# Two qkv blocks of the next image between the last turns of an image, and an own reciprocal root

## What is computed

```python
def _gn(v, G=32, eps=1e-5):
    g = v.reshape(B_, G, C_ // G, H_, W_)
    m = jnp.mean(g, axis=(2, 3, 4), keepdims=True)
    s = jnp.var(g, axis=(2, 3, 4), keepdims=True)
    return ((g - m) / jnp.sqrt(s + eps)).reshape(v.shape)

proj = xw @ W_qkv + b_qkv                   # q, k, v of every pixel
logit = jnp.einsum('npc,nqc->npq', q_win * SCALE, k_win)   # window means
topk_logit, r_idx = jax.lax.top_k(logit, TOPK)             # 4 windows of 49
attn = jax.nn.softmax(jnp.einsum('bmqc,bmkc->bmqk', q_h * SCALE, k_sel), axis=-1)
o = jnp.einsum('bmqk,bmkc->bmqc', attn, v_sel)
out = (o + lepe) @ W_o + b_o                # lepe: 3x3 depthwise conv of v
x = x + out
```

## Time and profile before

| | us |
|---|---|
| median of 3 runs | 3751.95 |
| lowest, highest | 3751.21, 3754.92 |
| the profiled execution's own time | 3752.41 |
| its span in the profile | 3750.6 |
| first layer, to about | 1650 |
| PE, DVE, ACT, POOL busy | 3507.4, 2372.2, 2143.5, 1659.6 |

### The profile page before, as it was taken

One profiled execution on the slowest core, in us unless ns is written; L12 is line 12 of the kernel. 1 busy time (PEld: TensorE's weight loads), 2 busy tenths in 40 slices (PEclk: granted clock), 3 DMA queues, 4 the chain that ended last, 5 costly groups with the idle time before them and its releaser, 6 DMA issues. The chain is left out here.

```text
span 3750.6 us, 107535 instructions
## 1 busy us (share of the span) xinstructions
PE 3507.4 (94%) x31974; PEld 2975.0 (79%) x31974; DVE 2372.2 (63%) x6267; ACT 2143.5 (57%) x5921; POOL 1659.6 (44%) x2575
## 2 busy tenths in 40 slices
PE   6989898989899999969999999999999969979999
PEld 4656565656566565669999999999999969979998
DVE  5868787777778786843333333333333359988898
ACT  5979797888888797944443333333333324345554
POOL 2736364645556464710003333333334436646665
PEclk8999999999999999989999999999999979989999
DMA  6232332323141423211110000000001200000000
GB/s 219 69 99 74 92 82 89 85 64 105 59 113 48 120 56 115 59 67 50 50 46 0 0 0 0 0 0 0 0 12 62 62 21 1 1 25 24 35 35 35
DMA packets 202870, 194.34 MB, mean 52 GB/s; under 512 B 35744, under 2 KB 191136, under 8 KB 199456
## 3 DMA queue, kind: packets, MB, share of 16 engines
q1 hardware_dynamic: 171168, 177.15, 15.2%
q10 hardware_dynamic: 31360, 12.87, 1.3%
HBM read 123.30 MB, written 66.58 MB: 51 GB/s over the span
## 5 line engine op out<-in xcount | busy, mean ns | idle before, releaser
L196 PE MATMUL bank<-h,w_hh 128*128 128x128 f32 x8032 | 933.8, 275 | 0.0
L196 PEld LDWEIGHTS bank<-h,w_hh 128*128 128x128 f32 x8032 | 917.0, 192 | 0.0
L241 ACT ACTIVATE h<-bank,bg 128x128 f32<-128x128 f32 x1008 | 370.1, 367 | 818.7 <-PE bank L196 818.6
L1582 ACT ACTIVATE Pr<-bank,nmx 128x256 f32<-128x256 f32 x1568 | 722.6, 477 | 110.4 <-DVE nmx L1700 96.7
L1521 POOL TENSOR_TENSOR Pr<-Pr,rden 128x768 f32<-128x768 f32 x392 | 574.7, 1466 | 389.4 <-DVE rden L1767 389.4
L1700 DVE TENSOR_REDUCE nmx<-bank 128x1 f32<-128x256 f32 x1568 | 556.2, 416 | 207.5 <-PE bank L1868 204.8
L287 DVE SCALAR_TENSOR_TENSOR inp<-bank,b_in,tz 128x256 f32<-128x256 f32 x196 | 85.8, 479 | 696.4 <-ACT tz L224 696.4
L1513 POOL COPY kg<-kT 128x64 f32 x1568 | 315.0, 244 | 341.3 <-DMA row<-ix 187.0
L1879 PE MATMUL bank<-ident,Pr 128*128 128x128 f32 x3136 | 449.8, 284 | 16.5 <-DVE Pr L1756 9.6
L1591 ACT ACTIVATE PT<-bank 128x512 f32<-128x512 f32 x784 | 427.2, 604 | 36.4 <-PE bank L1879 33.8
L1879 PEld LDWEIGHTS bank<-ident,Pr 128*128 128x128 f32 x3136 | 338.6, 142 | 116.0 <-issue 74.4
(11 more groups left out here) (265 smaller groups left out, 6497.9 us busy)
## 6 DMA issues: line engine op xcount, KB each, us to landing
v_rows<-v_padded SPq DMA_DIRECT2D x168, 232.0 KB, 3.3
vg<-v_windows SPq DMA_DIRECT2D x1176, 32.0 KB, 2.0
first_gates<-gate_sums SPq DMA_DIRECT2D x28, 512.0 KB, 2.6
gate_sums<-first_gates SPq DMA_DIRECT2D x28, 512.0 KB, 3.6
v_padded<-vpad SPq DMA_DIRECT2D x56, 232.0 KB, 2.1
X<-in_x SPq DMA_DIRECT2D x8, 1568.0 KB, 15.2
vg<-v_windows ACTq DMA_DIRECT2D x392, 32.0 KB, 2.7
x_backup<-X SPq DMA_DIRECT2D x8, 1568.0 KB, 6.0
```

Source lines behind the costliest of these rows:

```text
L196: ins = pe.matmul(bank[m][:, tt * COLS:(tt + 1) * COLS], w_hh[:, k, m * 128:(m + 1) * 128], prev[:, k, :], start=False, stop=(k == NH - 1) ...
L241: act.activation(h[:, 2 * q + tt, m, :], bank[m][:, tt * COLS:(tt + 1) * COLS], ACT.Tanh, bias=bg[:, 0, m:m + 1]).then_inc(s_h, 1)
L1582: act.activation(Pr[:, par, j, :], bank[j][:, 0:KEYS], ACT.Exp, bias=nmx[:, par, j:j + 1], accum_out=den[:, par, j:j + 1])\
```

## The change

- `xb` has a place of its own, 2 x 448 elements a partition, apart from `PT`.
- Blocks 0 and 1 of an image are normalised by GpSimd (`first_normed`, a tensor_scalar of 128x448), block 0 between its scaling of windows 47 and 48, block 1 behind window 48. Blocks 2 to 6 stay on ScalarE.
- TensorE runs q and k of block 0 of the next image ahead of attend 47, its v products behind turn 48, q and k of block 1 behind attend 48, and the output block 6 then. ScalarE and VectorE take the results out in the same places.
- The square root on ScalarE and the reciprocal are gone. VectorE starts from a shifted and subtracted bit pattern and refines it in three steps. All of it is done in the function `small`, just ahead of the reciprocal for GpSimd (L1767) in windows 40 to 47: two operations at 40, one at 41, one at 42, two at 43, three at 44 and 45, two at 46 and 47.
- The two sums that block 0 had on VectorE go to later blocks (three in block 1, two in 2 and 3); statistics of the next image's block 0 come last.
- On GpSimd, VectorE and TensorE all images are written out with constant semaphore values. ScalarE loops over images 0 to 6, with image 7 behind it. SyncE's code is the same.

```diff
-            xb = PT[:, 0, 0:2 * BLK].rearrange("p (s k) -> p s k", s=2)
+            xb = sb("xb", [C, 2, BLK])
...
-            SUMS_AT = {0: (0, 1), 1: (2, 3), 2: (4, 5), 3: (6,)}
+            SUMS_AT = {1: (0, 1, 2), 2: (3, 4), 3: (5, 6)}
-            MEAN_AT, VAR_AT = 39, 41
+            MEAN_AT, VAR_AT = 40, 42
...
                 dve.tensor_copy(im, bank[7][:, 0:1]).then_inc(s_id, 1)
-                dve.wait_ge(s_id, d0 + 1)
-                dve.tensor_tensor(it, mi[:, 0:1], im, ALU.subtract).then_inc(s_id, 1)
-                dve.wait_ge(s_id, d0 + 2)
-                dve.scalar_tensor_tensor(iv, it, it, mi[:, 1:2], ALU.mult, ALU.add).then_inc(s_id, 1)
+                dve.tensor_scalar(it, bank[7][:, 0:1], mi[:, 0:1], None, ALU.subtract).then_inc(s_id, 1)
+
+            def input_square(dve, m):
+                dve.wait_ge(s_id, m * IN_DVE + 2)
+                dve.tensor_scalar(iv, it, it, mi[:, 1:2], ALU.mult, ALU.add).then_inc(s_id, 1)
...
-            def input_root(act, m):
-                act.wait_ge(s_id, m * IN_DVE + 4)
-                act.activation(ir, iv, ACT.Sqrt).then_inc(s_ir, 1)
+            def input_guess(dve, m):
+                dve.wait_ge(s_id, m * IN_DVE + 4)
+                dve.tensor_scalar(ir.bitcast(U32), iv.bitcast(U32), 1, None, ALU.logical_shift_right).then_inc(s_id, 1)
+                dve.wait_ge(s_id, m * IN_DVE + 5)
+                dve.tensor_scalar(ir.bitcast(I32), ir.bitcast(U32), -1.0, float(0x5f3759df), ALU.mult, ALU.add).then_inc(s_id, 1)
+
+            def input_step(dve, m, i):
+                d0 = m * IN_DVE + 6 + 3 * i
+                dve.wait_ge(s_id, d0)
+                dve.tensor_scalar(it, iv, ir, ir, ALU.mult, ALU.mult).then_inc(s_id, 1)
+                dve.wait_ge(s_id, d0 + 1)
+                dve.tensor_scalar(it, it, -0.5, 1.5, ALU.mult, ALU.add).then_inc(s_id, 1)
+                if i < 2:
+                    dve.wait_ge(s_id, d0 + 2)
+                    dve.tensor_scalar(ir, ir, it, None, ALU.mult).then_inc(s_id, 1)
...
+                dve.wait_ge(s_id, m * IN_DVE + 14)
+                dve.tensor_scalar(A[:, bass.ds(m, 1)], it, ir, None, ALU.mult).then_inc(s_id, 1)
+                dve.wait_ge(s_id, m * IN_DVE + 15)
+                dve.tensor_scalar(Bb[:, bass.ds(m, 1)], im, A[:, bass.ds(m, 1)], -1.0, ALU.mult, ALU.mult).then_inc(s_id, 1)
...
+                    def first_normed(m, b):
+                        pool.wait_ge(s_id, m * IN_DVE + IN_DVE)
+                        pool.tensor_scalar(xb[:, b, :].rearrange("p (w r c) -> p w r c", r=ROWS, c=WIN),
+                                           xblk(m, b).rearrange("p (r w c) -> p w r c", r=ROWS, c=WIN),
+                                           A[:, bass.ds(m, 1)], Bb[:, bass.ds(m, 1)], ALU.mult, ALU.add).then_inc(s_xp, 1)
...
                         norm_first(P2 - 2, 1)
+                        if more:
+                            first_normed(following(n), 0)
                         norm_first(P2 - 1, 0)
+                        if more:
+                            first_normed(following(n), 1)
...
+                            small(w)
                             dve.wait_ge(s_ex, (n * P2 + w) * PAIRS + 4)
                             dve.reciprocal(rden[:, par, 0:3], den[:, par, 0:3]).then_inc(s_rd, 1)
                             between(w)
                         finish(P2 - 1, 0)
+                        if more:
+                            keys(following(n), 0)
                         attended(P2 - 2)
+                        if more:
+                            values(following(n), 0)
                         attended(P2 - 1)
-                        if more:
-                            input_scale(dve, following(n))
...
                             turn(w - 1, (w + 1) % 2)
+                        if more:
+                            queries_keys(following(n), 0)
                         attend(P2 - 2, 1, (P2 - 2) % 3, (P2 - 2) // 3)
                         turn(P2 - 1, 0)
+                        if more:
+                            values(following(n), 0)
+                            tokens(following(n), 0)
                         attend(P2 - 1, 0, (P2 - 1) % 3, (P2 - 1) // 3)
+                        if more:
+                            queries_keys(following(n), 1)
                         out(NBLK - 1, 0)
                         out(NBLK - 1, 1)
-                    with pe.Fori(0, B - 1) as n:
-                        image(n, True)
-                    image(B - 1, False)
+                    for n in range(B):
+                        image(n, n < B - 1)
```

More of the change, by code:

```diff
@@ L27 @@
 U32 = mybir.dt.uint32
+I32 = mybir.dt.int32
 ACT = mybir.ActivationFunctionType
@@ L69 @@
 GN_DVE, GN_PE = 11, 2
-IN_DVE = 12
+IN_DVE = 16
 def rsqrt_vector(e, r, v, tmp, done, d0):
@@ L1777, in image @@
                         dve.wait_ge(s_mvw, n + 1)
-                    with dve.Fori(0, B - 1) as n:
-                        image(n, True)
-                    image(B - 1, False)
+                    for n in range(B):
+                        image(n, n < B - 1)
                 @block.tensor
```

200 lines of the change are left out of this document (124 added, 76 removed).

## The result

| | before | after |
|---|---|---|
| median, us | 3751.58 (4 runs) | 3721.11 (4 runs) |
| lowest, highest | 3750.42, 3754.92 | 3718.89, 3723.68 |
| ratio, 95% interval | | 0.9913 (0.9901 to 0.9925) |
| span of the profiled execution | 3750.6 | 3720.8 |
| seven boundaries, us | 305.8 | 288.6 |

The kernel became faster by 30 us (28 to 37 by the interval), half of the 62 forecast; 3721 is 7 us above the upper end of the range, 3714. A boundary is counted as in the prediction, from the start of GpSimd's scaling of window 48 to that of the next image's window 0; a stretch of windows from the first scaling to the last. The last two lines of the table are added up from GpSimd's timeline.

A forecast was written before the change was run, and what follows sets the result against it. It saw time lost at seven image boundaries (306 us, no window worked on) and in two long windows. Terms 49.1 - 2.8 + 8.3 + 7.2 + 7.2 - 7 = 62.0 us took the time to 3690 us, range 3673 to 3714.

The forecast's parts named there:

- SyncE's part of the boundary: Image end: block 0's `vst` queues right behind the backup, lands at about 16, ScalarE waits 2; 0.3 us taken off.
- 36 to 37: Sign in the profile after: us from the scaling of window 48 to the next image's first, in place of 43.4.
- waits at `vst` for longer than 3 us: Sign of being wrong: ScalarE standing that long for the stored `vst` at the boundaries.
- The boundary term: Ends of images: block 2 starts 7.7 us earlier, less 0.6 and 0.3; seven boundaries and 1.5 more give 49.1 us.
- The stores behind the backup land late: Rival at the boundaries: `vst` lands 2 us later, each boundary is 2 us longer, 3704 us; chance 0.12.
- 3674 to 3702 from its bounds: Bounds of the sum: windows' terms at their ends, the boundary between 6 and 7.7; the sum as it stands has 0.62.
- Two long windows: Gaps 39 to 40 and 41 to 42: VectorE's stall goes, 8.3 us, and the half clock after it, 7.2 us.
- Constant waits: Windows of images written out on TensorE and VectorE, read from image 7 against image 2: 7.2 us gained, between 0 and 10.
- Small operations: Sixteen on VectorE in windows 40 to 47 delay the reciprocal, mainly in 44 and 45: -7 us, between 0 and 22.
- port rival: VectorE's small operations in windows 40 to 47 wait for GpSimd as L1351 did: 146 us lost, 3829 us; chance 0.03.
- GpSimd's operation: New normalising beside window 47: 0.86 us, delays VectorE's L1756 and the reciprocal for window 48 by 0.4; -2.8 us in all.
- The clock: TensorE at the boundaries: full clock expected to stay up, since its gaps of 1 to 3 us are filled; some 2 us each.

The follow-up runs named there:

- mean_from_psum: The kernel before, with the mean's subtraction read from PSUM as a tensor_scalar and the square as a tensor_scalar: 3743.1 us, ratio 0.9973 to the kernel before.
- vector_looped: The changed kernel with SyncE's images written out, but VectorE's images 0 to 6 a loop again: 3725.8 us, ratio 0.9918 to the kernel before.

## Why the prediction was wrong

**The step that failed** is SyncE's part of the boundary: "It lands at about 16, ScalarE wants it for block 2 at 13.9, and waits 2. ... I take off 0.3." The transfer was placed right behind the backup, without the branch between the two. At this boundary ScalarE could go on at 19.9, after 7.3 us of waiting, and TensorE after 4.3; at the others it was 6.0 to 6.3 and 3.1 to 3.2. Behind that TensorE ran at half its clock for 3 to 7 us. The very stall had been read in the profile: VectorE's 5.68 us "behind it, while the image's backup filled the transfer engines". It was taken for VectorE's and crossed out there, and SyncE, whose "code is the same", was not asked. Yet SyncE's branch sits one instruction behind the issue of that backup, and the change pulls the work that follows it forward by 9 us. With SyncE written out the sentence holds: `vst` goes at +16.2, block 4 at +17.6, the boundaries are 36.0, the "36 to 37" of the prediction. (The sign "waits at `vst` for longer than 3 us" was set too tight: 3.0 to 3.9 us are left there and do no harm.) The boundary term comes to 53.6 there (305.8 - 252.2), where 49.1 was forecast; the time is 3685.8, where 3690 was.

**A rival named it half.** "The stores behind the backup land late", at 2 us a boundary and 0.12, had the right place, but not the branch as the reason. Its price was mis-sized: the boundaries came out 4.5 us longer than forecast (41.2 - 36.7). With the true price it would have given 3722. The range is no better founded: "3674 to 3702 from its bounds" doesn't follow from the terms. With all of them at their ends they give 3671 to 3721, and that the upper end is the measured time is chance, since the missing term isn't among them.

**The other terms**, from the gaps between scalings in all eight images:
- Two long windows: 15.5 forecast, 16.2 measured in windows 39 and 41, less 1.0 in 40 and 42. mean_from_psum alone gives 13.7.
- Constant waits: 7.2 forecast, 7.6 measured in windows 4 to 38. It was read off from image 7. The gain is not VectorE's: in vector_looped it is 7.8. TensorE and VectorE alone gave 3.8 in the kernel before; that the rest is GpSimd's, which is written out too, wasn't tried.
- Small operations: -7 forecast, -7.5 measured, all of it in windows 43 to 46, 1.1 us an image. Half of that lies in one gap, from 43 to 44 (3.55 us in place of 3.02); the forecast had put it in 44 and 45. No stall of the port rival's kind is among them.
- GpSimd's operation: -2.8 forecast, +0.2 measured. VectorE's operation was held up by 0.43 us (0.78 against 0.35), as forecast. But GpSimd didn't wait longer: VectorE's reciprocal for window 48 comes 2.73 us behind the scaling of 47 (412.69 and 409.96), where it came 2.77 behind it before, and the gap from 47 to 48 is 3.08, before 3.12. The price of VectorE's delay was right, and there was slack ahead of the reciprocal that the forecast didn't see. The Trainium skill (SBUF — State Buffer, § Who interferes with whom) states the exclusion that the 0.78 shows. The Trainium skill's rate of 1.8 cycles an element (GPSIMD Engine Reference, § 3.1), an estimate of 0.67 us for the operation itself, is nearer to the measured 0.72 than the 0.86 taken from the scaling.
- First windows of an image: no term; 0.0 in all, but between 2.6 us better and 1.4 worse from image to image, with the clock.
- The first scaling of all comes 0.6 us later, forecast 0. Behind the last window some 2 us are lost (the last scaling is 32.1 us earlier, the program 29.8). Neither was looked into.

The clock behaved as forecast while TensorE had work. Where it fell at the boundaries, a wait stood ahead of it.

**What the mechanism is**, as far as the runs show it. A taken branch sends the engine for code, over the instruction queue: the packets are seen at 426 to 429 after, at 417 to 420 with little traffic. At every boundary of the changed kernel that queue moves two or three of them between 12 and 17 us after the last scaling; with SyncE written out it moves one or none. Written out on SyncE, the whole program has 23 packets fewer (111 against 134), about three for each pass of the loop; with VectorE looped again 35 more, five for each, of which some come ahead of the branch. Until the code is there the engine stands: 3.0 to 3.6 us with 0.45 MB of backup on the way, 5.4 to 6.6 with 1.57 MB (for SyncE from issue to issue, of which 0.6 are there without a branch). That the backup holds these packets up is inferred, from the times that go with the two amounts and from the first packets coming as the backup ends. The Trainium skill (Runtime: NRT & Kernel Launch, § Instruction fetch mechanics) says that a taken branch to a target outside the window of code that an engine holds forces a transfer of that code before it can go on. The traces agree, with the fall-through of vector_looped (0.22 us) as the counterpart; the page has no time for it, and nothing on other traffic. How much is left without any traffic, at this place, wasn't measured.

ScalarE loops over images 0 to 6 as well, and hardly stands at its branch: at this boundary of the changed kernel its last row in the loop is followed by xb of block 2 at once, and no packet of q14 moves from 411 to 421 (timeline, ScalarE). From row to row it takes 0.34 to 0.36 us at six boundaries, and 0.16 at the seventh, where the loop falls through, so the taken branch costs 0.2.

```profile
418.36 0.26 ACT L1585 ACTIVATE vst<-bank 64x128 f32<-64x128 f32 x1
418.70 0.76 ACT L1597 ACTIVATE xb<-X,Bb,A 128x448 f32 x1
```

The bodies differ in length. In one pass the timeline counts 519 instructions of VectorE (vector_looped) and 194 transfers of SyncE. ScalarE has 576, transfers included, but 48 of its windows go through an inner loop written for six, which leaves 114 in its code. Waits and register instructions come on top for all three, and no view counts them. The same section of the Trainium skill (Runtime: NRT & Kernel Launch, § Instruction fetch mechanics) gives an engine room for two blocks of 256 instructions, of which a new one is fetched ahead in order; a short body would stay inside, and a long one be fetched anew. That would fit the three, but no run varied the length of a body, so it is an explanation and not shown.

## What to carry to other kernels

SyncE and VectorE stand for 3 us at each taken branch here with 0.45 MB of transfers on the way, and for twice that with 1.57 MB; less than 0.45 MB wasn't measured. So look where each looping engine's branch lies, SyncE's too, and who waits for its first instruction behind it. When a change pulls work forward past such a place, a stall that was hidden comes out, so a stall read on one engine has to be asked of all the others that loop. And an engine's wait for a late result, even of a harmless store, blocks what stands behind it: place it by when the engine gets there, not by which window it is called.

## What was not expected

- One line that changes no work and no order, SyncE's loop over images, was worth 35 us in the changed kernel and 4 (1.5 to 8.6) in the kernel before.
- Loop and backup cost far more together than apart: 36.0 us a boundary without the loop, 36.5 without the backup (where the branch was passed before anyone needed it), 41.2 with both.
- A taken branch cost 3.0 to 6.6 us on SyncE and VectorE, and 0.2 on ScalarE.
- Five of the backup's seven pieces among the windows cost no time once SyncE no longer waited for their data (windows 1218.7 us, against 1224.8 without them); the backup between the stores of a boundary costs 29 us (whole) or 25 (in pieces) more than ahead of all stores.
- A stall of 0.9 us in one window brought half the clock two windows later (1.4 us, five images of eight); taking the stall away took both.
